# An opening rearranged: one W1 piece on another DMA queue, two square loads on ACT, and the rotation's signs inside its products

## What is computed

```
x_quat     = x.reshape(B, T, 4, 64)
x_filtered = ifft(fft(x_quat, axis=1) * spectral_gate).real   # the gate is one number per lane: a scaling
x_rotated  = hamilton(q_left_n, hamilton(x_filtered, conj(q_right_n)))
probs      = softmax(x_rotated @ Wr.T)
h          = gelu(x_rotated @ W1[7] + b1[7])
y          = (h @ W2[7] + b2[7]) * probs[:, 7:8]
out        = x + y
```

## Time and profile before

| | us |
|---|---|
| median of 3 runs | 102.66 |
| lowest, highest run | 102.07, 102.77 |
| the profiled execution | 102.56 |
| its span (first to last recorded work) | 100.7 |
| PE busy | 96.7 |
| DVE busy | 67.2 |
| ACT busy | 58.0 |

### The profile page before, as it was taken

One profiled execution on the slowest core, in us unless ns is written; L12 is line 12 of the kernel. 1 busy time (PEld: TensorE's weight loads), 2 busy tenths in 40 slices (PEclk: granted clock), 3 DMA queues, 4 the chain that ended last, 5 costly groups with the idle time before them and its releaser, 6 DMA issues.

```text
span 100.7 us, 1484 instructions
## 1 busy us (share of the span) xinstructions
PE 96.7 (96%) x516; PEld 81.6 (81%) x516; DVE 67.2 (67%) x137; ACT 58.0 (58%) x101; POOL 25.4 (25%) x20
## 2 busy tenths in 40 slices
PE   6899999999999999999999999999999999999980
PEld 7689888888888888878888888888888888888970
DVE  1669698799955699923231694699328697656560
ACT  0469899966849944923425955865509944443600
POOL 3223000000000000004999999994000000000000
PEclk9999999999999999999999999999999999999999
DMA  2979999998880000000000100001431810360014
GB/s 62 327 176 248 274 221 206 211 179 174 190 261 11 0 0 0 7 0 0 0 0 1 2 7 2 2 0 27 103 79 8 175 28 0 84 131 0 0 44 164
DMA packets 20822, 8.57 MB, mean 85 GB/s; under 512 B 17872, under 2 KB 19408, under 8 KB 20816
## 3 DMA queue, kind: packets, MB, share of 16 engines
q1 hardware_dynamic: 20096, 7.69, 35.6%
q10 hardware_dynamic: 720, 0.79, 2.5%
HBM read 6.36 MB, written 2.10 MB: 84 GB/s over the span
## 4 chain that ended last, share of the span: by engine, by line
PE 92%; DMA 2%; DVE 2%; DVEq 0%; issue 0%
PE pre L911 41%; PE acc L934 22%; PE acc L938 11%; PE acc L948 5%; PE acc L956 4%; PE pre L864 3%; PE acc L822 2%; DMA quats<-in_small 2%; PE lT_bank L854 2%; PE acc L952 1%; PE acc L950 1%; DVE y L715 1%; PE acc L839 1%; PE lT_bank L839 0%; DVEq L77 0%; PE acc L832 0%
## 5 line engine op out<-in xcount | busy, mean ns | idle before, releaser
L460 ACT ACTIVATE h_hi<-pre,quats 128x512 fp32r<-128x512 f32 x32 | 22.0, 689 | 30.7 <-PE pre L911 29.6
L648 DVE TENSOR_TENSOR h_lo<-h_all,h_hi 128x512 fp32r<-128x512 f32 x32 | 22.0, 689 | 21.0 <-ACT h_all L462 20.7
L934 PE MATMUL acc<-h_hi,w_parts 128*128 128x512 f32 x96 | 25.7, 389 | 0.0
L911 PE MATMUL pre<-xT_hi,w_hi 128*128 128x512 f32 x60 | 23.5, 392 | 0.0
L911 PE MATMUL pre<-xT_lo,w_hi 128*128 128x512 f32 x60 | 23.4, 390 | 0.0
L388 POOL TENSOR_TENSOR exps<-e_const,shifted 128x32 f32<-128x32 f32 x4 | 22.0, 5533 | 0.1
L462 ACT ACTIVATE h_all<-pre,quats 128x512 f32<-128x512 f32 x32 | 21.9, 683 | 0.0
L934 PEld LDWEIGHTS acc<-h_hi,w_parts 128*128 128x128 f32 x96 | 18.0, 188 | 3.7
L911 PE MATMUL pre<-xT_hi,w_lo 128*128 128x512 f32 x60 | 18.5, 390 | 0.0
L938 PE MATMUL acc<-h_lo,w_parts 128*128 128x512 f32 x48 | 14.8, 389 | 0.0
L911 PEld LDWEIGHTS pre<-xT_hi,w_lo 128*128 128x128 f32 x60 | 11.3, 188 | 2.4
(11 more groups left out here) (89 smaller groups left out, 92.0 us busy)
## 6 DMA issues: line engine op xcount, KB each, us to landing
x_sq<-in_x SPq DMA_DIRECT2D x12, 128.0 KB, 3.8
w<-in_W SPq DMA_DIRECT2D x4, 256.0 KB, 4.5
w_last<-in_W_last SPq DMA_DIRECT2D x4, 256.0 KB, 6.6
out<-out_sq SPq DMA_DIRECT2D x8, 128.0 KB, 2.8
x_sq<-in_x SPq DMA_DIRECT2D x8, 64.0 KB, 3.4
w_late<-in_W_late SPq DMA_DIRECT2D x4, 128.0 KB, 3.7
x_last<-in_x SPq DMA_DIRECT2D x1, 512.0 KB, 4.3
out<-out_sq SPq DMA_DIRECT2D x8, 64.0 KB, 2.2
```

What stands on the lines that cost most here:

```text
L460: nc.scalar.activation(h_hi[:, s, :], pre_bank(b, f)[:, :], ACT.Gelu, bias=b1_cols[:, f:f + 1]).then_inc(h_hi_ready, 1)
L648: nc.vector.tensor_tensor(h_lo[:, s, :], h_all[:, s, :], h_hi[:, s, :].bitcast(F32), ALU.subtract).then_inc(h_lo_ready, 1)
L911: last = nc.tensor.matmul(bank[:, :], w[:, k, cols], part_of_x[:, k, :], start=(n == 0), stop=(n == len(steps) - 1))
L934: nc.tensor.matmul(sums(b, k), w2_parts[:, f, i, k * P:(k + 1) * P], h_hi[:, s, :], start=(f == 0 and i == 0), stop=False)
```

## The change

- SP issues the second half of `w1_first` directly behind quats, in front of x_first. ACT issues only the first half.
- `load_first_squares` takes the engine and the quadrants as arguments. Of the four loads for the tokens 256 to 511 SP issues the quadrants 0 and 1, ACT 2 and 3, behind w1_second and in front of the small Gelu.
- `signed` and its semaphore are gone. `terms_of(k)` is now two instructions, each of which multiplies right_terms by one left component (a scalar per partition) and by the signs: one for the terms 1 to 3 of all four sums, one for term 0. `sums_of` waits for both. The squares for the norms stand at other places.

```
@@ queues @@
+        def load_first_squares(engine, h, quadrants):
+            for q in quadrants:
+                engine.dma_start(x_sq[0][q * SQ:(q + 1) * SQ, h * SQUARES // 2:(h + 1) * SQUARES // 2, :],
+                                 first_squares[h, q]).then_inc(first_sq_loaded[h], 16)
             sp.dma_start(quats[:, :], small).then_inc(q_loaded, 16)
+            sp.dma_start(w1_first[:, 1, :], W1_first[1]).then_inc(w1_first_loaded[1], 16)
             sp.dma_start(x_first[:, :, :], first_half).then_inc(first_x_loaded, 16)
-            load_first_squares(1)
+            load_first_squares(sp, 1, (0, 1))
@@ scalar @@
-            for k in range(KC):
-                act.dma_start(w1_first[:, k, :], W1_first[k]).then_inc(w1_first_loaded[k], 16)
+            act.dma_start(w1_first[:, 0, :], W1_first[0]).then_inc(w1_first_loaded[0], 16)
             act.dma_start(w1_second[:, :, :], W1_second).then_inc(w1_loaded[1], 16)
+            load_first_squares(act, 1, (2, 3))
             nc.scalar.activation(gelu_scratch[:, :], warm[:, :], ACT.Gelu)
@@ vector @@
             def terms_of(k):
-                dve.wait_ge(signed_ready, 1)
-                nc.vector.tensor_tensor(terms[:, 4 * k:4 * k + 4, :],
-                                        signed[:, k, :].rearrange("p (c t) -> p c t", t=4),
-                                        left_terms[:, k, :].unsqueeze(1).to_broadcast([P, 4, 4]),
-                                        ALU.mult).then_inc(terms_ready, 1)
+                right = right_terms[:, k, :].rearrange("p (c t) -> p c t", t=4)
+                sign = signs.rearrange("p (c t) -> p c t", t=4)
+                out = terms[:, 4 * k:4 * k + 4, :]
+                nc.vector.scalar_tensor_tensor(out=out[:, :, 1:4], in0=right[:, :, 1:4], scalar=left_terms[:, k, 1:2],
+                                               in1=sign[:, :, 1:4], op0=ALU.mult, op1=ALU.mult).then_inc(terms_ready, 1)
+                nc.vector.scalar_tensor_tensor(out=out[:, :, 0:1], in0=right[:, :, 0:1], scalar=left_terms[:, k, 0:1],
+                                               in1=sign[:, :, 0:1], op0=ALU.mult, op1=ALU.mult).then_inc(terms_ready, 1)
             def sums_of(k):
-                dve.wait_ge(terms_ready, k + 1)
+                dve.wait_ge(terms_ready, 2 * (k + 1))
```

More of the change, by code:

```diff
@@ L109, in adaln_ffn @@
         minus_half = sb("minus_half", [P, 2, KC])
-        signed = sb("signed", [P, KC, 16])
         terms = sb("terms", [P, KC * 4, 4])
@@ L208, in adaln_ffn @@
         lane_eye_ready = sem("lane_eye_ready")
-        signed_ready = sem("signed_ready")
         squares_ready = sem("squares_ready")
@@ L328, in _ @@
             load_w2(3)
-            load_first_squares(0)
+            load_first_squares(sp, 0, range(QUADS))
             sp.dma_start(b2_all[:, :], b2.to_broadcast([P, C])).then_inc(b2_loaded, 16)
@@ L538, in _ @@
             dve.wait_ge(q_loaded, 16)
-            nc.vector.tensor_tensor(signed[:, :, :], right_terms, signs.unsqueeze(1).to_broadcast([P, KC, 16]),
-                                    ALU.mult).then_inc(signed_ready, 1)
+            terms_of(0)
             dve.wait_ge(eps_set, 1)
@@ L543, in _ @@
                                     ALU.mult).then_inc(squares_ready, 1)
-            terms_of(0)
+            sums_of(0)
             nc.vector.tensor_tensor(squares[:, :, 3:7], right_terms[:, :, ::4], right_terms[:, :, ::4],
                                     ALU.mult).then_inc(squares_ready, 1)
-            sums_of(0)
             dve.wait_ge(lane_eye_ready, 1)
```

## The result

| | changed | before |
|---|---|---|
| median, us | 102.97 (19 runs) | 102.32 (19 runs) |
| lowest, highest | 102.08, 104.91 | 101.76, 102.77 |
| ratio, 95% interval | 1.0043 [1.0022, 1.0064] | 1 |

The changed kernel is slower by 0.4%, within the range and within 1%, but not "no change": the interval leaves 1 out. It was timed twice more beside the kernel before: 1.0064 [1.0035, 1.0094] and 1.0025 [0.9998, 1.0053]. These ratios leave out executions more than 1.5% above the fastest of their kernel; for this change those are part of the story, so I count them: at 104 us or above (a line drawn after the result was seen) lie 8 of 43 executions of the changed kernel and 5 of 150 of the kernel before.

The account below looks back on a forecast made before the run. PE bounds the kernel, through the moment it may begin the first fold. The rotation's 0.05 us off the profiled 102.56 gives 102.51, off the median 102.66 gives 102.61: forecast 102.6, "no change", range 101.9 to 103.1.

Parts of the forecast that it names:

- The bound: PE, busy 96.7 of 100.7 us: the end is set by when it may begin the first fold, 3.98 us.
- the cover of x_first: x_first on SP lands at 4.7 us, at most 5.3; PE can load it from 5.44: cover 0.7, worst 0.1.
- W1's piece: Second half piece on SP lands between 3.8 and 4.4 us instead of about 4.5; by itself gives nothing.
- The squares: Square loads from SP and ACT: the last landed at 6.6 us, DVE turned them at 6.88; hidden, cost nothing.
- The rotation: On DVE, two waiting steps instead of three: R(0) 0.07 us earlier, of which the end gets 0.05.
- R(1): On DVE, starts 0.78 us after R(0) instead of 0.62; cover before the fold's third record 0.10, the thinnest.
- ACT: Two square issues move its small Gelu's end from 3.77 to 4.64 us; cover 0.6 until 5.24, cost nothing.
- rival A: Square issues cost more on ACT, which becomes late for the fold's end: 103.2 or 104.1 us; chance 0.08.
- Rival D: W1's second half piece had held the fold; its earlier landing gives up to 0.2 to 0.3: 102.3 us; chance 0.08.
- Rival B: The two STTs on DVE run one behind the other: 102.6 to 102.7 us; chance counted within the forecast's 0.72.
- Rival C: PE's clock rises at another moment: 101.7, at most 101.4, or 103.1 us if later; chance 0.12.
- The numbers: Forecast 102.6 us, range 101.9 to 103.1; chances 0.06 faster by over 1%, 0.05 slower, 0.89 the rest.

Follow-up runs that it names:

- x_on_act: The changed kernel with x_first as ACT's second DMA, ahead of w_second: 102.44 us against 102.33 of the kernel before; again, 102.55 against 102.53.
- rotation_only: The kernel before with only the new rotation on DVE, all DMAs as before: 102.40 us against 102.44, ratio 1.0009.
- squares_only: The kernel before with only two of the four square loads moved to ACT, behind w_second: 102.63 us against 102.44, ratio 1.0015.
- w1_second_behind: The kernel before, but SP issues quats, W1's second piece, x_first, w_second, squares; ACT only w_first's first half: 102.92 us against 102.33, ratio 1.0059.
- w1_piece_only: The kernel before with only W1's second half piece moved to SP, in front of x_first: 102.80 us against 102.44, ratio 1.0035.
- before_warm5: The kernel before with five warm-up matmuls instead of six, no DMA touched: 103.72 us against 102.32, ratio 1.0128.
- after_side: The changed kernel as it is, timed again on one chip with the kernel before: 102.83 us against 102.53, ratio 1.0025.
- columns_front: The kernel before with the 24 KB load of column_quats put between quats and x_first on SP: 105.70 us against 102.44.

## Why the prediction was wrong

*The bound.* That "one moment sets the end: when PE may begin the first fold" holds for that one execution. It was read from a profile in which the clock rose at 6.3 us. Where it rises earlier, the fold is done at 5.4 to 5.5 (x_on_act), and the landings of x_first and of the squares come next, or that of w_second, which led the chain of rotation_only. In squares_only the chain led through x_sq, and PE waited 0.3 for xT_hi.

*The step that failed* is the cover of x_first: "moves back by one issue, 0.46, and lands at 1.2 + 0.46 + 3.0 = 4.7", "at most 5.3", "cover 0.7, at worst 0.1". I took the landing time, 3.0, to be the transfer's own, and shifted it with the issue. Measured behind an issue at 1.65: 4.1, 4.3 and 4.7 in the three profiles of the changed kernel, so 5.7, 6.0 and 6.4. x_first was late by 1.5 to 2.2 us instead of 0.46. At first I looked for the cause in w_second, which moved ahead; w1_second_behind shows that x_first is late without it as well. That x_first's move makes most of the loss is shown by w1_piece_only, which brings it, and by x_on_act, which takes it away and differs from the changed kernel in the place of x_first alone. Why the landing moved so far is open: the place on the queue, the time of issue and the bytes each miss some of the profiles.

*W1's piece* on SP was forecast to land between 3.8 and 4.4; it came at 4.1 to 4.7 in the changed kernel, and that "it keeps the piece from being late" bought nothing that shows: on ACT, with the new rotation, it cost nothing either (rotation_only).

*The squares* were forecast to land by 6.6 and to be "hidden". In the profiled execution DVE waited for them until 7.4, behind a PE that was late itself. With the squares alone moved they landed at 7.1, and the loss of PE was 0.3 in that profile and not clear of noise in the median.

*The rotation.* The mechanism was right (two steps instead of three), the size off: 0.03 instead of 0.07. An STT of this size takes 0.23 and the next starts 0.15 behind it, not 0.11 as behind a plain product. R(1) came 0.82 after R(0), forecast 0.78, within its cover.

*ACT* was right to 0.01 us, so rival A fell. Rival D was not put to a clean test: in the three profiles of the changed kernel W1's piece landed at 4.1, 4.4 and 4.7 where it had landed at about 4.5, and no gain is seen. Rival B didn't occur. Rival C named the clock as the source of spread, but "the same spread will be in both kernels" was wrong: 8 of 43 against 5 of 150. before_warm5 shows that a longer pause in front of the fold is enough to raise the times. That the x_first wait, behind the fold, made the changed kernel's upper group is not shown, and the record speaks against it as the whole cause: in after_side the clock was low until about 10 us with PE's break ahead of x_first under 0.1, and in w1_piece_only PE waited 1.7 for x_first with the clock up behind it, and none of its 12 executions reached 104. What made that group stays open.

*The numbers.* 102.97 lies in the range and within 1%. The chances gave 0.05 to a loss above 1%, and nothing was forecast for one of 0.4 to 0.6%, which the many runs could tell from zero.

## What to carry to other kernels

In the opening of a short kernel the order of the DMAs over the queues is a resource of its own: moving one load ahead of another can cost far more than the issue time that it takes (here 1.5 to 2.2 us for an issue of 0.46). A landing time in a profile belongs to the whole order of loads in that profile; don't shift it with the issue, nor take it from the bytes or the place alone. If its cover is thin, look at more than one profile. And where the clock rises at different moments from run to run, one profile shows the cover of a transfer only for that moment; ask what would come last if PE were twice as fast up to there.

## What the runs showed of the hardware

- The DMA engines can stand idle for 0.5 us (share 0.02 from 3.0 to 3.5 in w1_second_behind) with an issued DMA in the queue.
- Where a load of 256 KB stands on its queue doesn't alone say when it lands. x_first took 3.0 to 3.8 us from its issue as second on SP and 4.0 to 5.2 as third, 6.1 behind a load of 24 KB; as second on ACT 3.4, 3.5 and 4.1, as third 4.3. w_second took 3.4 to 5.3 as second on ACT and 3.5 to 4.5 as third, and 6.3 when 24 KB were put into SP's queue.
- A landing isn't a constant of the program: x_first took 4.1, 4.3 and 4.7 in three executions of one and the same program.
- What PE does ahead of the fold acts on the clock: with a pause of 0.3 us in the profile 5 of 150 executions were at 104 us or above; with 0.7 us, by one matmul on zeros less, all 6 lay above 102.9 and the profiled one had the lower level until nearly 10 us. With a pause filled by matmuls on zeros the group vanished (0 of 12 where 8 of 12 had been). A wait of 1.7 us behind the fold did not bring the lower level in w1_piece_only; behind one of 2.7 in columns_front the granted clock was 0.50 from 8 to 10 us, the lower level, though the fold before it had run at the higher one in part (1.58 us for its four records).
